# Moving row loads and feature stores from ScalarE's queue to SyncE's in a graph-attention and feed-forward kernel

## The chip, the cores and the metric

The kernel runs on one core of a Trainium2 chip. The metric is the device time of one execution in microseconds (us). The engines are TensorE (PE in the profile), VectorE (DVE), ScalarE (ACT), GpSimd (POOL) and SyncE (SP). SyncE does no arithmetic: it waits for semaphores and issues DMAs, one after the other, in program order. ScalarE can issue DMAs too, between its own instructions.

## What is computed

```python
x = x + gnn(layernorm(x), edge_index, ...)      # two graph-attention layers, 1250 nodes, 21250 edges
x = x + ffn(layernorm(x), ...)                  # GELU feed-forward, six class tokens with routed experts

def gat_layer(x, W, att_src, att_dst, bias, src, dst, heads, out_ch):
    h = (x @ W.T).reshape(n, heads, out_ch)
    e = leaky_relu(a_src[src] + a_dst[dst], 0.2)
    alpha = segment_softmax(e, dst)             # over the edges that end in one node
    return segment_sum(alpha * h[src], dst) + bias
```

The first layer has 8 heads of 128 channels (x is 1250x768, W1 is 1024x768).

## The kernel before

The edges are turned into a dense matrix. For each pair of nodes the kernel counts the edges and keeps the logarithm of the count; a softmax over a dense 1250x1250 matrix of logits plus log counts then replaces the segment operations. The 1250 nodes are worked on in `NT` = 10 tiles of `NP` = 125 rows.

The change lies in the first stage, roughly the first 145 us. For each tile t this stage does the following.

- **Rows.** `load_x(t)` loads 125 rows of x into `xin[t % 2]`. ScalarE takes the mean (`means`, L882), subtracts it (`centre`, L891) and sums the squares (L895). When L895 of tile t is done the semaphore `sq_ready` stands at t, and `xin[t % 2]` may be loaded again, with tile t+2. So `load_x(t + 2)` waits for `sq_ready` t.
- **Turning and products.** TensorE transposes the centred rows (`turn`, L1281), ScalarE copies them out of PSUM (`rows_turned`, L836 to L839), and `products(t)` (L1351) multiplies them with W1 in three passes.
- **Features.** `features_out(t)` (L864, L870) takes the result out of PSUM into `h1st[t % 2]`, with the semaphore `h1_out`. Its first piece frees the PSUM bank in which `products(t + 1)` begins (`h1_piece`). `store_h1(t)` stores `h1st[t % 2]` to the scratch tensor h1_d in DRAM; `features_out(t + 2)` waits until it has landed.
- **Counts.** `count_edges(t)` (L1268) counts the edges of a tile on TensorE with one-hot matrices that VectorE makes (L1968). `log_counts(t)` (L847) has ScalarE write the logarithms to `LCw[t % 2]`; VectorE mends them (`mend`, L1988, semaphore `lc_done`). SyncE stores them to DRAM (`store_lc(t)`, L478, 1250 pieces of 500 bytes, because the columns are re-ordered on the way) and loads them back row-wise (`load_lc(t)`, L485).

Two waits matter below. The first is at the head of `log_counts(t)`, a wait for the store of two tiles before, since it writes the same buffer:

```python
act.wait_ge(cnt_full, t + 1)
freed(act, lc_stored[t % 2], TWO * (t // 2))
```

The second is the program order of each engine: nothing is reordered by a scheduler, every engine runs the list written out by hand. On ScalarE one turn i of the loop at L939 is `features_out(i - 1)`, `rows_turned(i + 1)`, `means` and `centre` of tile i + 2, and `log_counts` at places set by hand: in turn 5 that of tile 5 comes right after `features_out(4)`, and that of tile 6 comes last, right ahead of `features_out(5)` in turn 6.

Each transfer of 125 rows is issued as two DMAs (`ROWS`: 112 rows and 13 rows).

Of the kernel before, what the change touches and what calls it, by code (L numbers as in the profile page):

```python
# [34 lines left out]
NP = 125  # L35
NT = N // NP
# [45 lines left out]
ROWS = ((0, CUT), (CUT, NP))  # L82
# [79 lines left out]
def gnn_ffn_kernel(nc, x, src_cols, dst_cols, dst_rows, W1, W1T, as1T, ad1T, b1c, W2, W2T, as2T, ad2T,  # L162
                   b2, fc1T, fc1b, fc2T, fc2b, gate_pair, atom_inT, atom_inb, atom_outT, atom_outb,
                   balance, out):
    h1_d = nc.dram_tensor("h1_scratch", (N, HC), F32).ap()
# [5 lines left out]
    with ctx:  # L171
        def sb(name, shape, dt=F32, where=ctx):
            return where.enter_context(nc.sbuf_tensor(name, shape, dt))

        def sem(name):
            return ctx.enter_context(nc.semaphore(name))
# [104 lines left out]
        xin = [sb("xin0", [NP, D], F32, p1)]  # L281
# [22 lines left out]
        h1st = [sb("h1st0", [NP, HC], F32, p1)]  # L304
# [105 lines left out]
        mean_step, sq_ready, h1_piece = (sem(n) for n in ("mean_step", "sq_ready", "h1_piece"))  # L410
        x_in = [sem(f"x_in{p}") for p in range(2)]
        stat_step, rstd_ready, xn_ready, xt_full, xT_ready = (
            sem(n) for n in ("stat_step", "rstd_ready", "xn_ready", "xt_full", "xT_ready"))
        logit_full, logit_rows, column_full, logit_done, h1_full, h1_out = (
            sem(n) for n in ("logit_full", "logit_rows", "column_full", "logit_done", "h1_full", "h1_out"))
        h1_stored = [sem(f"h1_stored{p}") for p in range(2)]
# [51 lines left out]
        def _(sp):  # L468
            def load_x(t):
                for a, b in ROWS:  # L470
                    sp.dma_start(xin[t % 2][a:b, :], x[t * NP + a:t * NP + b, :]).then_inc(x_in[t % 2], 16)

            def store_lc(t):

                sp.wait_ge(lc_done, t + 1)
                flat = lc_d.rearrange("n m -> (n m)")[t * NP * N:(t + 1) * NP * N]
                for a, b in ROWS:
                    sp.dma_start(flat.rearrange("(w p r) -> p w r", w=SUB, p=NP)[a:b, :, :],  # L478
                                 LCw[t % 2][a:b, :].rearrange("p (w r) -> p w r", w=SUB)).then_inc(lc_stored[t % 2], 16)

            def load_lc(t):

                sp.wait_ge(lc_stored[t % 2], TWO * (t // 2 + 1))
                for a, b in ROWS:
                    sp.dma_start(LC[a:b, t, :], lc_d[t * NP + a:t * NP + b, :]).then_inc(lc_in[t // 2], 16)  # L485

            def load_w2n(k):
                sp.dma_start(w2n_sb[:, k, :], W2[k * 128:(k + 1) * 128, :]).then_inc(w2n_in, 16)

# [15 lines left out]
            sp.dma_start(fc1b_sb[:, :], fc1b).then_inc(bias_in, 16)  # L505
            sp.wait_ge(sq_ready, 1)
            load_x(3)
            sp.wait_ge(wattp, 1)
            for k in range(KD):
                load_w2n(k)  # L510
            store_lc(0)
            for i in range(1, 8):
                store_lc(i)
                load_lc(i - 1)


            def load_features(q, h):
# [286 lines left out]
        def _(act):  # L804
# [26 lines left out]
            def rows_turned(t):  # L831
                p = t % 2
                act.wait_ge(xt_full, t + 1)
                if t > 2:
                    act.wait_ge(h1_full, t - 1)
                act.copy(xT[p][:, 0:4, :], bank[3][:, 0:4 * NP].rearrange("p (k n) -> p k n", k=4))  # L836
                act.copy(xT[p][:, 4:6, :], bank[4][:, 0:2 * NP].rearrange("p (k n) -> p k n", k=2))
                act.copy(xT_hi[p][:, 0:4, :], bank[3][:, 0:4 * NP].rearrange("p (k n) -> p k n", k=4))
                act.copy(xT_hi[p][:, 4:6, :], bank[4][:, 0:2 * NP].rearrange("p (k n) -> p k n", k=2)  # L839
                         ).then_inc(xT_ready, 1)  # L840

            def log_counts(t):
                act.wait_ge(cnt_full, t + 1)
                freed(act, lc_stored[t % 2], TWO * (t // 2))
                for b in range(3):
                    c0, c1 = b * 2 * GW, min((b + 1) * 2 * GW, N)
                    last = act.activation(LCw[t % 2][:, c0:c1], bank[b][0:NP, 0:c1 - c0], ACT.Ln,  # L847
                                          bias=tiny[:, 0:1], scale=2.0)
                last.then_inc(ln_done, 1)

            def features_out(t):
                act.wait_ge(h1_full, t + 1)
                freed(act, h1_stored[t % 2], TWO * (t // 2))
                pieces = THIRDS if t < FUSED else LAST_HALVES if t == NT - 1 else HALVES
                scale = 1.0
                if t in CENTRED:
                    act.wait_ge(rstd_ready, 2 * t + 1)
                    scale = rstd[:, t:t + 1]
                if t == NT - 1:
                    act.activation(h1s[0][:, t, :], bank[pieces[0][0]][0:NP, 0:C], ACT.Copy, scale=1.0  # L860
                                   ).then_inc(head_in[0], TWO)
                for b, c0, c1 in pieces:
                    c1 = min(c1, HC)
                    c = act.activation(h1st[t % 2][:, c0:c1], bank[b][0:NP, 0:c1 - c0], ACT.Copy, scale=scale)  # L864
                    if c0 != pieces[-1][1]:
                        c.then_inc(h1_piece, 1)
                if 0 < t < FUSED:
                    freed(act, rows_full, t - 1)
                    freed(act, col_done, t - 1)
                    c = act.activation(cols[t % 2][:, :], bank[5][0:NP, LOGIT0:LOGIT0 + 2 * H], ACT.Copy, scale=scale)  # L870
                c.then_inc(h1_out, 1)

            def centre_first():
                act.wait_ge(stat_step, 3)
                act.activation(xn[0][:, :], xin[0][:, :], ACT.Identity, bias=nmr[0][:, 0:1], scale=1.0).then_inc(xn_ready, 1)

            def means(t):
                p = t % 2
                act.wait_ge(x_in[p], TWO * (t // 2 + 1))
                act.wait_ge(stat_step, 4)  # L880
                freed(act, xt_full, t - 1)
                act.activation(xn[p][:, :], xin[p][:, :], ACT.Identity, bias=0.0, scale=1.0,  # L882
                               accum_out=mv[p][:, 0:1]).then_inc(mean_step, 1)
                act.wait_ge(mean_step, 2 * t - 1)
                act.activation(stats[p][:, 0, 0:1], mv[p][:, 0:1], ACT.Copy, scale=-1.0 / D).then_inc(mean_step, 1)
                act.wait_ge(mean_step, 2 * t)

            def centre(t):

                p = t % 2  # L890
                act.activation(xn[p][:, :], xin[p][:, :], ACT.Identity, bias=stats[p][:, 0, 0:1], scale=1.0  # L891
                               ).then_inc(xn_ready, 1)
                act.wait_ge(xn_ready, t + 1)
                freed(act, rstd_ready, 2 * t - 4)
                act.activation(xin[p][:, :], xn[p][:, :], ACT.Square, accum_out=mv[p][:, 1:2]).then_inc(sq_ready, 1)  # L895
# [7 lines left out]
            def store_h1(t):  # L903

                act.wait_ge(h1_out, t + 1)
                for a, b in ROWS:
                    act.dma_start(h1_d[t * NP + a:t * NP + b, :], h1st[t % 2][a:b, :]).then_inc(h1_stored[t % 2], 16)

            def load_x(t):

                act.wait_ge(sq_ready, t - 2)
                for a, b in ROWS:
                    act.dma_start(xin[t % 2][a:b, :], x[t * NP + a:t * NP + b, :]).then_inc(x_in[t % 2], 16)

            centre_first()
            first_turned()
            act.copy(iota2[:, :, 1], iota1[:, :]).then_inc(consts_made, 1)
# [12 lines left out]
            log_counts(0)  # L930
            means(2)
            centre(2)
            store_h1(0)
            load_x(4)
            rows_turned(2)
            means(3)
            centre(3)
            load_x(5)
            for i in range(2, NT):  # L939
                features_out(i - 1)  # L940
                if i in (2, 5):
                    log_counts({2: 1, 5: 5}[i])
                if i + 1 < NT:
                    rows_turned(i + 1)
                if i in (4, 7, 8):
                    log_counts({4: 4, 7: 8, 8: 9}[i])
                if i + 2 in CENTRED:
                    means(i + 2)
                    centre(i + 2)
                    if i + 4 < NT:  # L950
                        load_x(i + 4)
                elif i + 2 < NT:
                    normalise(i + 2)
                store_h1(i - 1)
                if FUSED <= i + 3 < NT:
                    means(i + 3)
                    squares(i + 3)
                if i in (2, 3, 5, 6):
                    log_counts({2: 2, 3: 3, 5: 6, 6: 7}[i])
                if i == NT - 2:  # L960
                    act.activation(early_exp[:, :], tiny[:, :], ACT.Exp)
# [1577 lines left out]
```

## Time and profile before

| | |
|---|---|
| median of 3 runs | 699.24 us (699.22 to 701.13) |
| the profiled execution, its own time | 699.48 us |
| span of its profile, first to last instruction | 697.5 us |
| TensorE busy | 685.4 us, 98% of the span |
| VectorE busy | 511.8 us, 73% |
| ScalarE busy | 441.1 us, 63% |
| DMA queue of SyncE (q1), share of 16 DMA engines | 32.2% |
| DMA queue of ScalarE (q10), share of 16 DMA engines | 6.0% |

The span is one execution, measured from its first to its last instruction; the execution's own time has about 2 us more around it. Busy shares are averages over stages with different limits. In the rows further down, ACTq and SPq are the DMA issues of ScalarE and of SyncE, and a time is microseconds from the start of the span.

### The profile page before, as it was taken

The page shows a single profiled execution, that of the slowest core. Times are in us where ns is not written, and L with a number is a line of the kernel's source. Part 1 is how long each engine was busy: PE and PEld are TensorE (multiplying, and loading weights), DVE is VectorE, ACT ScalarE, POOL GpSimd, SP SyncE. Part 2 cuts the span into 40 slices and gives each one's busy share as a digit, 9 for nine tenths or more (in the row PEclk, how much of TensorE's full clock was granted, in tenths as well). Part 3 has the DMA queues.
Part 4 walks back from the last instruction along what each step waited for, and adds up shares of the span by engine and source line. Part 5 has one row for each costly group of instructions (what it writes and reads, how often), then busy time and mean ns, then how long its engine had stood idle before and what let it go on. Part 6 is the DMA issues. An engine that isn't in the chain of part 4 may idle for free.

```text
span 697.5 us, 13734 instructions
## 1 busy us (share of the span) xinstructions
PE 685.4 (98%) x4749; PEld 644.8 (92%) x4749; DVE 511.8 (73%) x866; ACT 441.1 (63%) x900; POOL 126.3 (18%) x150
## 2 busy tenths in 40 slices
PE   7999999999999999999999999999999999999997
PEld 6799999889999999999999899999998999999997
DVE  7888875999899999999998854434668643837332
ACT  5767676388999999999999744454261424422202
POOL 2324120001021212112121000000242330333302
PEclk9999999999999999999999999999999999999999
DMA  8877886868434434343323231101963544315102
GB/s 286 252 255 211 198 220 161 205 194 275 82 72 84 101 57 99 70 81 90 58 22 79 73 106 60 59 1 52 318 206 117 159 137 162 95 59 188 32 23 69
DMA packets 54430, 88.37 MB, mean 127 GB/s; under 512 B 17763, under 2 KB 37081, under 8 KB 54378
## 3 DMA queue, kind: packets, MB, share of 16 engines
q1 hardware_dynamic: 43798, 65.69, 32.2%
q0 software_dynamic: 6080, 8.17, 7.4%
q10 hardware_dynamic: 4500, 13.82, 6.0%
q8 instruction: 31, 0.51, 0.3%
q14 instruction: 21, 0.17, 0.1%
HBM read 68.09 MB, written 15.33 MB: 120 GB/s over the span
## 4 chain that ended last, share of the span: by engine, by line
PE 87%; DVE 7%; ACT 2%; issue 2%; DVEq 1%; DMA 1%; POOL 0%; SPq 0%; ACTq 0%
PE bank L1495 19%; PE bank L1635 13%; PE bank L1456 12%; PE bank L1559 12%; PE bank L1351 10%; PE bank L1739 4%; PE bank L1711 3%; PE bank L1268 2%; PE bank L1613 2%; PE bank L1765 1%; DVE x2f L2392 1%; PE bank L1501 1%; PE bank L1502 1%; ACT w_hi L1054 1%; PE bank L1796 1%
## 5 line engine op out<-in xcount | busy, mean ns | idle before, releaser
L1495 PE MATMUL bank<-PT,h1s 125*128 125x250 f32 x660 | 147.5, 374 | 0.0
L1495 PEld LDWEIGHTS bank<-PT,h1s 125*128 125x128 f32 x660 | 121.2, 190 | 13.6
L2157 DVE SCALAR_TENSOR_TENSOR L<-asb,nad 125x1250 f32<-125x1250 f32 x80 | 121.3, 1552 | 1.5 <-DMA asb<-src_logit_rows 0.7
L2168 DVE CUSTOM_DVE_ANT_0 L<-L,LC 125x1250 f32<-125x1250 f32 x80 | 113.7, 1453 | 1.3
L969 ACT ACTIVATE L<-L,nm 125x1250 f32<-125x1250 f32 x80 | 109.7, 1373 | 6.1 <-DVE nm L2168 4.8
L1456 PE MATMUL bank<-ident,L 125*125 125x125 f32 x800 | 94.0, 273 | 0.0
L1456 PEld LDWEIGHTS bank<-ident,L 125*125 125x125 f32 x800 | 91.1, 189 | 0.8 <-issue 0.4
L990 ACT COPY PT<-bank 125x500 f32<-125x500 f32 x165 | 83.8, 619 | 2.7 <-PE bank L1456 2.7
L777 POOL DMA_DIRECT2D PT_diff<-PT x34 | 28.4, 837 | 158.9 <-ACT PT L990 158.9
L1968 DVE TENSOR_TENSOR hot<-iota,edges 125x750 f16<-125x750 f16 x100 | 46.9, 540 | 6.5 <-PE bank L1268 4.4
L1635 PE MATMUL bank<-h_hi,PT_hi 125*125 125x384 f32 x200 | 41.5, 350 | 0.0
L1635 PE MATMUL bank<-h_lo,PT_hi 125*125 125x384 f32 x200 | 40.5, 342 | 0.0
L1111 ACT ACTIVATE L<-L,nm 125x1250 f32<-125x1250 f32 x10 | 13.4, 1341 | 42.4 <-DVE nm L2312 42.4
L745 POOL TENSOR_TENSOR x<-x,b_sb 125x768 f32<-125x768 f32 x10 | 20.0, 1996 | 102.0 <-DMA fc2b_sb<-in_fc2b 92.3
L1635 PE MATMUL bank<-h_hi,PT_lo 125*125 125x384 f32 x200 | 38.1, 336 | 0.0
L1635 PEld LDWEIGHTS bank<-h_hi,PT_hi 125*125 125x125 f32 x200 | 34.0, 185 | 2.5 <-ACT PT_hi L1119 0.7
L1635 PEld LDWEIGHTS bank<-h_hi,PT_lo 125*125 125x125 f32 x200 | 35.2, 185 | 0.0
L1061 ACT ACTIVATE hT<-hT,b_sb x64 | 19.5, 387 | 24.7 <-DVE hT L2219 24.7
L2244 DVE COPY as2c<-bank 125x1 f32<-125x1 f32 x10 | 1.6, 159 | 45.6 <-ACT h_hi L1074 45.6
L1635 PEld LDWEIGHTS bank<-h_lo,PT_hi 125*125 125x125 f32 x200 | 34.9, 186 | 0.0
L2369 DVE TENSOR_TENSOR x2f<-bank,x2f 125x384 f32<-125x384 f32 x20 | 10.2, 552 | 29.6 <-PE bank L1739 27.9
L1559 PE MATMUL bank<-w_hi,h1Tt_hi 128*125 128x384 f32 (+1 forms) x160 | 31.0, 344 | 0.6 <-ACT w_hi L1054 0.5
(289 smaller groups left out, 1340.6 us busy)
## 6 DMA issues: line engine op xcount, KB each, us to landing
asb<-src_logit_rows SPq DMA_DIRECT2D x14, 416.5 KB, 3.5
atom_w<-in_atom_inT SPq DMA_DIRECT2D x5, 1152.0 KB, 12.2
atom_w<-in_atom_outT SPq DMA_DIRECT2D x5, 1152.0 KB, 9.7
log_count_scratch<-LCw SPq DMA_DIRECT2D x10, 546.9 KB
LC<-log_count_scratch SPq DMA_DIRECT2D x10, 546.9 KB
LCt<-log_count_scratch SPq DMA_DIRECT2D x10, 546.9 KB
h_scratch<-h1st ACTq DMA_DIRECT2D x10, 448.0 KB
PT_diff<-PT POOLq DMA_DIRECT2D x34, 122.1 KB, 3.0
```

Of the source, the lines that this page charges most:

```text
L777: pool.dma_start(PT_diff[p][:, :].bitcast(F32), PT[p][:, PART + 1, :], accum_op=ALU.add).then_inc(lower_moved[p], 16)
L969: e = act.activation(L[r][:, :], L[r][:, :], ACT.Exp, bias=nm[q][:, t:t + 1], scale=-1.0, accum_out=den[q][:, t:t + 1])
L990: act.copy(PT[(k - lag) % 2][:, 2 * b:2 * b + 2, :], turned[0:NP, 0:2 * GW].rearrange("p (s n) -> p s n", s=2)).then_inc(tb_evac, 1)
L1351: mm = pe.matmul(bank[b][0:NP, 0:c1 - c0], rows[t % 2][:, k, :], weights[:, k, c0:c1], start=(part == 0 and k == 0), stop=(part == 2 and k ...
L1456: mm = pe.transpose(bank[turned_bank(first, k - lag, b)][0:NP, (2 * s + j) * NP:(2 * s + j + 1) * NP], L[(2 * (k - lag) + j) % RING][:, (2 ...
L1495: mm = pe.matmul(sums, h1s[q][:, s, :], PT[p][:, s, :], start=(s == (0 if plain else PART + 2)), stop=(plain and s == NT - 1))
L1559: mm = pe.matmul(bank[2 * p + b][0:NP, 0:w], rows[p][:, k, :], weights[:, k, c0:c0 + w], start=(part == 0 and k == 0), stop=(part == 2 and ...
L1635: mm = pe.matmul(bank[2 + 2 * j + b][0:NP, 0:HALF], rows[:, s, j * NP:(j + 1) * NP], features[:, s, b * HALF:(b + 1) * HALF], start=(term ...
L1739: mm = pe.matmul(bank[down_bank(i, j) + b][0:NP, 0:HALF], rows[:, m, j * NP:(j + 1) * NP], weights[:, m, b * HALF:(b + 1) * HALF], start=( ...
L1968: made = dve.tensor_tensor(hot[w][:, :, :, :], iota2[:, w * NP:(w + 1) * NP, :].unsqueeze(1).to_broadcast([CE, VISIT, NP, 2]), edges[t % 2 ...
L2157: dve.scalar_tensor_tensor(L[s % RING][:, :], asb[q][0:NP, 1, :], nad1[:, ds(h, 1), t:t + 1].rearrange("p h t -> p (h t)"), asb[q][0:NP, 0 ...
L2168: dve.tensor_tensor_reduce(out=L[s % RING][:, :], in0=L[s % RING][:, :], in1=LC[:, t, :], scale=-1.0, scalar=-FLOOR, op0=ALU.add, op1=ALU.min,
```

## The change

ScalarE's `load_x` is gone: the row loads of tiles 4 to 9 are issued by SyncE, with the same condition on `sq_ready`. The feature stores of tiles 0 to 6 are issued by SyncE as well, with the same condition on `h1_out`; those of tiles 7 to 9 stay on ScalarE. SyncE's list of log-count stores and loads is woven together with them.

```diff
+            def load_next_x(t):
+                sp.wait_ge(sq_ready, t - 2)
+                load_x(t)
+
+            def store_h1(t):
+                sp.wait_ge(h1_out, t + 1)
+                for a, b in ROWS:
+                    sp.dma_start(h1_d[t * NP + a:t * NP + b, :], h1st[t % 2][a:b, :]).then_inc(h1_stored[t % 2], 16)
+
...
             sp.wait_ge(sq_ready, 1)
             load_x(3)
+            store_h1(0)
+            load_next_x(4)
             sp.wait_ge(wattp, 1)
             for k in range(KD):
                 load_w2n(k)
+            load_next_x(5)
+            store_h1(1)
             store_lc(0)
-            for i in range(1, 8):
-                store_lc(i)
-                load_lc(i - 1)
+            for i in range(2, 9):
+                if i + 4 < NT:
+                    load_next_x(i + 4)
+                if 2 < i < 8:
+                    store_h1(i - 1)
+                store_lc(i - 1)
+                load_lc(i - 2)
...
-            store_h1(0)
-            load_x(4)
             rows_turned(2)
             means(3)
             centre(3)
-            load_x(5)
             for i in range(2, NT):
                 features_out(i - 1)
...
                 if i + 2 in CENTRED:
                     means(i + 2)
                     centre(i + 2)
-                    if i + 4 < NT:
-                        load_x(i + 4)
                 elif i + 2 < NT:
                     normalise(i + 2)
-                store_h1(i - 1)
+                if i > 7:
+                    store_h1(i - 1)
```

On SyncE, before, the store of tile 3's log counts (`LCw1`) and that of tile 4 (`LCw0`) stand next to each other, with the load of tile 2 between them:

```order
L478 DMA log_count_scratch<-LCw1 112x10x125 [waits lc_done]
L478 DMA log_count_scratch<-LCw1 13x10x125
L485 DMA LC<-log_count_scratch 112x1250 [waits lc_stored0]
L485 DMA LC<-log_count_scratch 13x1250
L478 DMA log_count_scratch<-LCw0 112x10x125 [waits lc_done]
L478 DMA log_count_scratch<-LCw0 13x10x125
```

In the changed kernel (its line numbers differ: L471 loads rows of x, L494 stores features) the same place reads as follows, from the load of tile 8's rows to the feature store of tile 4; the store of tile 4's log counts comes right after it:

```order
L471 DMA xin0<-in_x 112x768 [waits sq_ready]
L471 DMA xin0<-in_x 13x768
L494 DMA h1_scratch<-h1st1 112x1024 [waits h1_out]
L494 DMA h1_scratch<-h1st1 13x1024
L478 DMA log_count_scratch<-LCw1 112x10x125 [waits lc_done]
L478 DMA log_count_scratch<-LCw1 13x10x125
L485 DMA LC<-log_count_scratch 112x1250 [waits lc_stored0]
L485 DMA LC<-log_count_scratch 13x1250
L471 DMA xin1<-in_x 112x768 [waits sq_ready]
L471 DMA xin1<-in_x 13x768
L494 DMA h1_scratch<-h1st0 112x1024 [waits h1_out]
L494 DMA h1_scratch<-h1st0 13x1024
```

The log-count stores of tiles 3 and 4 now each stand behind a wait for `sq_ready` and four more issues.

On ScalarE, before, turn 5 goes from the squares of tile 7 (L895) through four issues to the means of tile 8, its squares (L900) and the log counts of tile 6:

```order
L895 ACTIVATE xin1,mv1<-xn1 125x768 [waits rstd_ready,xn_ready]
L913 DMA xin1<-in_x 112x768 [waits sq_ready]
L913 DMA xin1<-in_x 13x768
L907 DMA h1_scratch<-h1st0 112x1024 [waits h1_out]
L907 DMA h1_scratch<-h1st0 13x1024
L882 ACTIVATE xn0,mv0<-xin0 125x768 [waits xt_full,stat_step,x_in0]
L885 ACTIVATE stats0<-mv0 125x1 [waits mean_step]
L900 ACTIVATE xn0,mv0<-xin0,stats0 125x768 [waits rstd_ready,mean_step]
L847 ACTIVATE LCw0<-bank0,tiny 125x500 [waits lc_stored0,cnt_full]
```

In the changed kernel the same instructions follow each other without the issues (L912 is the old L895, L864 the old L847):

```order
L912 ACTIVATE xin1,mv1<-xn1 125x768 [waits rstd_ready,xn_ready]
L899 ACTIVATE xn0,mv0<-xin0 125x768 [waits xt_full,stat_step,x_in0]
L902 ACTIVATE stats0<-mv0 125x1 [waits mean_step]
L917 ACTIVATE xn0,mv0<-xin0,stats0 125x768 [waits rstd_ready,mean_step]
L864 ACTIVATE LCw0<-bank0,tiny 125x500 [waits lc_stored0,cnt_full]
```

The wait for `lc_stored0` in front of the log counts has stayed where it was.

## Rows read from the trace of the kernel before

**Rows 1.** The page: busy time of TensorE, share of the span, instructions.

```profile
PE 685.4 (98%) x4749; PEld 644.8 (92%) x4749; DVE 511.8 (73%) x866; ACT 441.1 (63%) x900; POOL 126.3 (18%) x150
```

**Rows 2.** Busy time of each engine by stretch, then TensorE clock, DMA share, GB/s.

```profile
20.00:43.00 23.00, 21.24 (x223) 18.58 (x222) 17.32 (x39) 15.85 (x34) 6.68 (x6) 1.00 0.83 273
...
43.00:150.00 107.00, 106.17 (x856) 98.15 (x854) 88.04 (x167) 69.70 (x146) 19.55 (x16) 1.00 0.74 192
```

**Rows 3.** Timeline of TensorE at tile 6: start us, us, what.

```profile
91.56 0.81 PE L1281 MATMUL bank<-ident,xn 125*128 125x125 f32 x6
92.46 3.10 PE L1351 MATMUL bank<-w_hi,xT_hi 128*125 128x352 f32 x18
...
97.44 0.29 PE L1259 MATMUL bank<-iota,zeros 125*125 125x16 f16 x3
...
103.30 0.80 PE L1281 MATMUL bank<-ident,xn 125*128 125x125 f32 x6
```

**Rows 4.** Timeline of ScalarE, with its DMA issues (ACTq), turns 4 to 6.

```profile
76.10 0.79 ACTq L913 DMA_DIRECT2D xin<-in_x  x2
76.93 0.81 ACTq L907 DMA_DIRECT2D h_scratch<-h1st  x2
...
80.28 1.60 ACT L847 ACTIVATE LCw<-bank,tiny 125x500 f32<-125x500 f32 x3 [0.42 <-PE bank L1271]
...
86.19 0.18 ACT L895 ACTIVATION_READ_ACCUMULATOR xin<-xn 125x1 f32 x1
86.40 0.79 ACTq L913 DMA_DIRECT2D xin<-in_x  x2
87.22 0.80 ACTq L907 DMA_DIRECT2D h_scratch<-h1st  x2
88.15 0.85 ACT L882 ACTIVATE xn<-xin 125x768 f32<-125x768 f32 x1 [1.78 <-issue]
...
90.29 1.58 ACT L847 ACTIVATE LCw<-bank,tiny 125x500 f32<-125x500 f32 x3
91.76 1.42 ACT L864 ACTIVATE h1st<-bank,rstd 125x352 f32<-125x352 f32 x3
```

**Rows 5.** Timeline of SyncE: log-count stores of tiles 3, 4, 5 and 6.

```profile
69.63 0.93 SPq L478 DMA_DIRECT2D log_count_scratch<-LCw  x2
...
77.96 1.66 SPq L478 DMA_DIRECT2D log_count_scratch<-LCw  x2
...
87.00 0.96 SPq L478 DMA_DIRECT2D log_count_scratch<-LCw  x2
...
98.50 0.95 SPq L478 DMA_DIRECT2D log_count_scratch<-LCw  x2
```

**Rows 6.** DMA packets of 76.1:85.9, of 85.9:88.1, of 86.4:95.6, of 98.5:104.5.

```profile
DMA packets 1748, 2.16 MB, mean 220 GB/s; under 512 B 1371, under 2 KB 1371, under 8 KB 1747
...
DMA packets 56, 0.16 MB, mean 71 GB/s; under 512 B 10, under 2 KB 10, under 8 KB 56
...
DMA packets 1769, 2.29 MB, mean 248 GB/s; under 512 B 1363, under 2 KB 1363, under 8 KB 1767
...
DMA packets 1389, 1.14 MB, mean 190 GB/s; under 512 B 1287, under 2 KB 1287, under 8 KB 1388
```

**Rows 7.** Timeline of VectorE: tile 3's log counts are mended.

```profile
68.14 1.45 DVE L1988 SCALAR_TENSOR_TENSOR LCw<-LCw 125x1250 f32<-125x1250 f32 x1
```

**Rows 8.** Timeline of ScalarE, turn 2 to 3.

```profile
52.86 1.61 ACT L847 ACTIVATE LCw<-bank,tiny 125x500 f32<-125x500 f32 x3 [3.64 <-PE bank L1271]
54.81 1.42 ACT L864 ACTIVATE h1st<-bank,rstd 125x352 f32<-125x352 f32 x3 [0.34 <-PE bank L1351]
```

**Rows 9.** Timeline of TensorE at the start, and the last stretch by windows.

```profile
1.54 4.64 PE L1232 MATMUL bank<-ident 128*128 128x128 f32 x26 [1.54 <-POOL ident L693]
...
7.87 1.04 PE L1232 MATMUL bank<-ident 128*128 128x128 f32 x8
...
694.00:697.50 3.50, 0.00 (x0) 0.00 (x0) 0.55 (x2) 0.00 (x0) 0.00 (x0) 1.00 0.38 112
```

More of the change, by code:

```diff
@@ L907, in store_h1 @@
                     act.dma_start(h1_d[t * NP + a:t * NP + b, :], h1st[t % 2][a:b, :]).then_inc(h1_stored[t % 2], 16)
[L909 to L913, printed above, removed]
             centre_first()
```

## The prediction

> **What bounds the kernel now.** I read the page first: TensorE is busy for 685.4 of 697.5 us, so only idle time of TensorE can be won, and any new idle time is lost for good [rows 1]. Next I read the busy time by stretch, for the stage that the change touches. From 43 to 150 us TensorE is busy for 106.17 of 107 us; from 20 to 43 us for 21.24 of 23 [rows 2]. The whole stage holds 0.83 + 1.76 = 2.6 us to win. Then I read the timelines of ScalarE, SyncE and TensorE side by side, looking for places where one of them has just enough slack. The reader is to see two.
>
> The first is the edge between tiles 5 and 6. TensorE starts the products of tile 6 at 92.46 [rows 3], and needs for that the first piece of `features_out(5)`, which ScalarE begins at 91.76 [rows 4]. Between them lies the piece itself (1.42 / 3 is about 0.5 us) and some 0.2 us. So TensorE is hard behind ScalarE here. Ahead of that piece ScalarE has no idle time: `log_counts(6)` runs from 90.29 to 91.8, right up to it [rows 4]. Whatever delays `log_counts(6)` delays TensorE by the same.
>
> The second is the log-count buffer, of which there are two. `log_counts(5)`, at 80.28, may start when the store of tile 3 has landed, and `log_counts(6)`, at 90.29, when that of tile 4 has [rows 4]. Now these stores are issued at 69.63 and 77.96 [rows 5], as soon as the values are mended (tile 3 at 68.14 + 1.45 = 69.6 [rows 7]). They are done long before they are needed: the one of tile 4 by 85.9, since of the packets under 512 B 1371 start from 76.1 to 85.9 (1250 are the store's, the rest completion writes and strays) and only 10 in the 2.2 us after [rows 6].
>
> **The change part by part.** It removes 26 issues from ScalarE (two for each of 6 loads and 7 stores). At 0.79 to 0.81 us for a pair [rows 4] that is 13 x 0.8 = 10.4 us. Most of it lies in front of a wait for TensorE anyway. The clearest place is turn 5: four issues from 86.40 to 88.02 hold up the means of tile 8 by 1.78 us [rows 4]. Without them `log_counts(6)` could begin at 88.5. It gains TensorE nothing, since `features_out(5)` needs TensorE's own products of tile 5, which end when the turning at 91.56 starts [rows 3]. I cost the removal at 0.
>
> It adds the same 26 issues to SyncE, and that is no cost by itself: SyncE is idle for most of the stage. What costs is the order. `store_lc(3)` stood behind nothing; now it stands behind `load_next_x(8)`, which waits for `sq_ready` 6, that is for the moment 76.1 at which ScalarE issued this load before [rows 4]. Behind that come two issues of x and two of the feature store, 0.8 us each pair, so the store of tile 3 leaves at 77.7 instead of 69.63. In the same way `store_lc(4)` stands behind `load_next_x(9)`, which waits for `sq_ready` 7.
>
> Let L be the time from the issue of the row load to the end of the log-count store behind it. The trace has this group of three transfers (rows, features, log counts) twice. From 76.1 to 85.9 it took 9.8 us [rows 4, 6]; the second begins at 86.40, with the store at 87.00, and its 500-byte packets are through by 95.6 (1363), which makes 9.2 [rows 4 to 6]. A store with little beside it went from 98.50 to 104.5, 6.0 us [rows 5, 6]; 1.6 us behind the row load that makes L at least 7.6. I take 9.2, because the group of three is what will run, and the second had nothing held back within it.
>
> The steps are then:
>
> 1. Store 3 ends at 76.1 + L = 85.3. `log_counts(5)`, due at 80.28, starts 5.0 us late. TensorE doesn't feel it yet: the next thing it needs is tile 7, centred, at 91.56 [rows 3]; ScalarE is done with that tile at 86.4 now [rows 4], so by 91.4 then.
> 2. Everything behind it on ScalarE is 5.0 late, `sq_ready` 7 too: it comes at 86.4 + 5.0 = 91.4. This holds `load_next_x(9)`, and with it `store_lc(4)`, on SyncE.
> 3. Store 4 ends at 91.4 + 9.2 = 100.6. `log_counts(6)`, due at 90.29, starts 10.3 us late. The 1.7 us of issues that ScalarE no longer makes are swallowed by this wait.
> 4. `features_out(5)` begins at 102.1 and TensorE stands from about 92.4 to 102.8: **10.3 us**. In general the stall is 2L - 8.1, so 7.1 us at L = 7.6 and 11.5 at 9.8.
>
> What is late next: SyncE's `store_h1(5)` and `store_lc(5)` follow `features_out(5)`, 1.7 us after its start, and end some 8.5 to 10 us after it. `log_counts(7)` takes 1.6 more, up to 11.6, and `features_out(6)` is due after 11.7 (a tile of TensorE, 91.56 to 103.30 [rows 3]). That just fits. The same holds a tile further, for `normalise(9)`. Early in the stage the store of tile 0's log counts now queues behind the feature store of tile 1 and must land by 52.86, with 0.34 us to spare before TensorE is touched [rows 8]. For these three near misses together I take **0.5 us**, and 0 to 2 as bounds.
>
> A third term is TensorE's clock. The rows show a granted clock of 1.00, that is 2.4 GHz, in both stretches [rows 2], and it also stayed there during the 3.5 us at the end in which TensorE did nothing [rows 9]. No row shows what 10 idle microseconds do. At the very start 26 transposes took 4.64 us (178 ns each), and later 8 took 1.04 (130 ns) [rows 9]; a start like that costs 26 x 48 ns = 1.2 us, and a stretch of 4.64 us at half speed can cost at most 2.3. I take **1.0 us**, bounds 0 and 2.3. The Trainium skill says (TensorE: Matmul & The Clock Gate, Part 1) that an array that has idled falls back to 1.2 GHz and gets 2.4 GHz again only after sustained work; by that rule alone the fall is sure, and the term would be at its full 1.2 or more instead of 1.0.
>
> A rule speaks for the other side. The row load and the feature store had a queue of their own beside the store of the log counts, and the three together took 9.2 to 9.8 us against 6.0 for the store alone [rows 6], so the two queues already shared one transfer capacity. The Trainium skill says the same (DMA: Bandwidth & Descriptors, Issuing engines are not separate DMA queues): DMAs of different engines run on the same 16 DMA engines, and spreading them only saves issue time. Read alone it would have this change cost nothing and give ScalarE its 10.4 us; it is silent on waits in the issuing engine's own list, where my 10.3 us come from.
>
> Sum: 10.3 + 0.5 + 1.0 = 11.8 us on the profiled execution's 699.48 us, 711.3. The median of before is 0.24 lower, so 711.0.
>
> **The rivals.**
>
> *Only one link bites.* If ScalarE's wait in step 1 were short (L near 5), step 3 would nearly vanish: 2 x 5 - 8.1 = 1.9 us, 701. It needs a store that lands 3.4 us after its issue; the lone one took 6.0 [rows 6]. 5%.
>
> *The stores stay hidden, nothing changes.* This is so for L below 4.05, or if the delay of step 1 were made up by ScalarE before `sq_ready` 7. ScalarE has 0.42 us of idle time ahead of `log_counts(5)` [rows 4], and its instructions from there to 86.4 follow one another. The time would be 699 to 700. 6%.
>
> *Faster: ScalarE was the hidden brake.* Here TensorE's small gaps come from ScalarE being held up by its issues, as in the 1.78 us at 88.15 [rows 4]. The price is bounded by the idle time of the stage, 0.83 us after 43 and 1.76 before [rows 2]: 696.7 to 698.5. It decides if no store is late, so from L below 4.05 as well, and to be seen at all it would need most of the 2.6 us. 3%.
>
> *The clock falls and the queue is slower.* With one queue instead of two in flight, L may pass 9.8; at 10.5 the stall is 12.9, with 2.3 for the clock and 1 for near misses 715.4. 10%.
>
> My forecast (a stall of 7 to 12 us at the edge of tiles 5 and 6) has 76%.
>
> **How the numbers follow.** The likeliest value is 711.0. The forecast's own range is L from 7.6 to 9.8 with the smallest and the largest other terms: 699.2 + 7.1 = 706.3 and 699.2 + 11.5 + 3.8 = 714.5. To leave no more than 2 in 10 out I go a little beyond on both sides, 705 to 715. A change of 0.3%, 2.1 us, is about what a measurement can tell from none here. Faster holds 0.03; the hidden case and part of the one-link case give same 0.08; the rest, 0.89, is slower.
>
> **What the profile after would show.** Step 1: SyncE's store of tile 3 at about 77.7, and ScalarE's `log_counts(5)` near 85, with idle time ahead of it. Step 2: the row load of tile 9 on SyncE near 91. Step 3: `log_counts(6)` near 100 with 6 us or more of idle time before it. Step 4: one gap of TensorE of about 10 us between the turning of tile 7 (the transposes that start near 91.6) and the products of tile 6, and busy time of TensorE otherwise as before; the granted clock in the windows behind the gap tells the third term. I'd be wrong if `log_counts(5)` started by 82, if TensorE's gap lay elsewhere, or if the stretch after 150 us were longer by more than the clock explains.

## The result, and the profile after

The changed kernel takes 712.7 us (median of 5 runs, 712.4 to 712.98) against 699.71 us (5 runs) for the one before: ratio 1.0184, with an interval of 1.0173 to 1.0195. Its profiled execution took 712.54 us with a span of 710.7, that is 13.1 us and 13.2 us more than the one before. The first operation of the attention stage on TensorE starts 13.14 us later (149.26 us instead of 136.12), so nearly all of the loss lies ahead of that point.

The page of the changed kernel answers to [rows 1], its busy time by stretch to [rows 2].

```profile
PE 690.1 (97%) x4749; PEld 649.0 (91%) x4749; DVE 512.0 (72%) x866; ACT 441.1 (62%) x900; POOL 125.9 (18%) x150
```

```profile
20.00:43.00 23.00, 21.18 (x223) 18.55 (x221) 17.32 (x39) 15.50 (x35) 6.91 (x6) 1.00 0.84 287
43.00:150.00 107.00, 97.12 (x741) 91.17 (x742) 75.33 (x151) 56.97 (x123) 18.92 (x16) 0.95 0.67 169
```

From 43 to 150 us TensorE is now idle for 9.9 of 107 us instead of 0.8, and its granted clock has fallen from 1.00 to 0.95. The busy time of the whole page has grown by 4.7 us with the same 4749 instructions: the same work ran slower somewhere.

SyncE's timeline, with its DMA issues (SPq), shows the two links of the chain. Columns: start us, duration us, what. Line 471 is the row load, 494 the feature store, 478 the log-count store.

```profile
75.96 0.76 SPq L471 DMA_DIRECT2D xin<-in_x  x2
76.77 0.78 SPq L494 DMA_DIRECT2D h_scratch<-h1st  x2
77.60 1.83 SPq L478 DMA_DIRECT2D log_count_scratch<-LCw  x2
...
91.10 0.76 SPq L471 DMA_DIRECT2D xin<-in_x  x2
91.90 0.79 SPq L494 DMA_DIRECT2D h_scratch<-h1st  x2
92.73 1.96 SPq L478 DMA_DIRECT2D log_count_scratch<-LCw  x2
```

The log-count store of tile 3 left at 69.63 before, that of tile 4 at 77.96 [rows 5]. Now they leave at 77.60 and 92.73, each behind a row load that waits for ScalarE. ScalarE's timeline, answering to [rows 4], shows what that does to `log_counts(5)`, `log_counts(6)`, `features_out(5)` and, for tile 6's store, `log_counts(8)`.

```profile
84.98 1.60 ACT L864 ACTIVATE LCw<-bank,tiny 125x500 f32<-125x500 f32 x3 [5.26 <-DMA log_count_scratch<-LCw]
...
100.56 1.60 ACT L864 ACTIVATE LCw<-bank,tiny 125x500 f32<-125x500 f32 x3 [7.36 <-DMA log_count_scratch<-LCw]
102.04 1.42 ACT L881 ACTIVATE h1st<-bank,rstd 125x352 f32<-125x352 f32 x3
...
126.00 1.60 ACT L864 ACTIVATE LCw<-bank,tiny 125x500 f32<-125x500 f32 x3 [6.64 <-DMA log_count_scratch<-LCw]
```

The time in brackets is the idle time ahead, with what ended it: three times it is the landing of a log-count store. Before, 80.28 and 90.29 stood where 84.98 and 100.56 stand now, with 0.42 us of idle time and none. ScalarE's chain of waits sums it up.

```profile
ACT LCw L864 <- DMA log_count_scratch<-LCw: 19.3, 3, 7.4
```

And TensorE's timeline answers to [rows 3].

```profile
80.54 3.14 PE L1358 MATMUL bank<-w_hi,xT_hi 128*125 128x352 f32 x18
88.21 0.37 PE L1318 MATMUL bank<-ident,cols 125*8 125x125 f32 x1 [4.53 <-ACT xT_hi L856]
88.23 4.47 PE L1358 MATMUL bank<-w_lo,xT_hi 128*125 128x352 f32 x18
...
97.49 0.81 PE L1288 MATMUL bank<-ident,xn 125*128 125x125 f32 x6
102.75 5.54 PE L1358 MATMUL bank<-w_hi,xT_hi 128*125 128x352 f32 x18 [4.46 <-ACT h1st L881]
...
128.57 0.86 PE L1288 MATMUL bank<-ident,xn 125*128 125x125 f32 x6 [0.52 <-ACT xn L839]
```

The reader is to see two gaps, not one: 4.53 us inside the products of tile 5 and 4.46 us ahead of those of tile 6. Behind each stands a pass of 18 products that is slow: 4.47 and 5.54 us, where the kernel before took 3.12 and 3.10 for the same passes. The windows give the clock behind the second gap.

```profile
92.00:105.00 13.00, 8.54 (x71) 8.30 (x70) 4.85 (x11) 5.61 (x15) 1.11 (x4) 0.86 0.68 179
104.00:108.00 4.00, 4.00 (x15) 3.93 (x15) 0.00 (x0) 3.94 (x10) 0.00 (x0) 0.50 0.85 239
110.00:131.00 21.00, 20.39 (x192) 19.79 (x191) 14.43 (x28) 9.67 (x22) 2.27 (x2) 1.00 0.67 164
```

The granted clock of 0.50 is the lower of TensorE's two levels, 1.2 GHz. The sum closes. The products of tile 6 start at 102.75 instead of 92.46, 10.29 us late: 4.53 + 4.46 us of idle time and 4.47 - 3.12 = 1.35 us of slow clock behind the first gap make 10.3. Behind the second gap the clock adds 5.54 - 3.10 = 2.4. Ahead of the transposes at 128.57 TensorE waits 0.5 more. That makes 13.2.

The first gap comes from these two lines of TensorE's `logit_turn(t)`, which `products(5)` calls for t = 4 behind its first part:

```python
pe.wait_ge(h1_out, t + 1)
...
pe.wait_ge(xT_ready, t + 3)
```

`xT_ready` 7 means that `rows_turned(6)` is done, and on ScalarE that stands behind `log_counts(5)`. Before, the last cast of `rows_turned(6)` started at 82.94 and the transpose followed at 83.64; now 87.65 and 88.21.

### The profile page after: what moved, and what is told of

It is laid out like the page before. It is cut to its first block, busy times and chain, and to the rows that moved or that the text cites. A ratio compares the mean times of both kernels' runs of the same rounds, so it can differ in the third digit from the quotient of the medians.

```text
span 710.7 us, 13734 instructions
## 1 busy us (share of the span) xinstructions
PE 690.1 (97%) x4749; PEld 649.0 (91%) x4749; DVE 512.0 (72%) x866; ACT 441.1 (62%) x900; POOL 125.9 (18%) x150
## 4 chain that ended last, share of the span: by engine, by line
PE 82%; DVE 7%; DMA 3%; ACT 3%; issue 2%; DVEq 1%; SPq 1%; POOL 0%; ACTq 0%
PE bank L1502 19%; PE bank L1642 13%; PE bank L1463 12%; PE bank L1566 12%; PE bank L1358 7%; PE bank L1746 4%; PE bank L1718 3%; DMA log_count_scratch<-LCw 3%; PE bank L1620 2%; PE bank L1772 1%; DVE x2f L2399 1%; PE bank L1275 1%; PE bank L1508 1%; PE bank L1509 1%; ACT w_hi L1061 1%
## 5 line engine op out<-in xcount | busy, mean ns | idle before, releaser
L1358 PE MATMUL bank<-w_hi,xT_hi 128*125 128x352 f32 (+2 forms) x150 | 31.1, 360 | 5.6 <-ACT h1st L881 4.5
L864 ACT ACTIVATE LCw<-bank,tiny 125x500 f32<-125x500 f32 (+1 forms) x30 | 16.1, 611 | 31.5 <-DMA log_count_scratch<-LCw 19.3
## 6 DMA issues: line engine op xcount, KB each, us to landing
atom_w<-in_atom_inT SPq DMA_DIRECT2D x5, 1152.0 KB, 13.2
```

The lines of the kernel that those rows point to most:

```text
L1358: mm = pe.matmul(bank[b][0:NP, 0:c1 - c0], rows[t % 2][:, k, :], weights[:, k, c0:c1], start=(part == 0 and k == 0), stop=(part == 2 and k ...
```

## The experiments

**1. Is it the order on SyncE, or the move itself?** `k1_counts_first` keeps every moved issue on SyncE and only turns the order within a turn round.

```diff
             for i in range(2, 9):
-                if i + 4 < NT:
-                    load_next_x(i + 4)
-                if 2 < i < 8:
-                    store_h1(i - 1)
                 store_lc(i - 1)
                 load_lc(i - 2)
+                if 2 < i < 8:
+                    store_h1(i - 1)
+                if i + 4 < NT:
+                    load_next_x(i + 4)
```

Expected: 

> All row loads and feature stores stay on SyncE as in the change, but in each turn SyncE's log-count store and load come first, then the feature store, then the row load. Theory 1 (the loss is the wait for sq_ready and h1_out that stands in front of the log-count stores in SyncE's list): the store of tile 3 leaves near 69.6 and that of tile 4 near 78 us again, no late log_counts, no gap of TensorE, granted clock 1.00 throughout; 699.7 us, within 1 us. Rival 2 (one queue in place of two is slower for the same transfers): a loss stays, 703 us or more. Rival 3 (ScalarE freed of 26 issues gains something once the stores are in time): 698 us or less.

Measured: 699.21 us (12 runs, 699.04 to 700.13) against 699.56, ratio 0.9993 (0.9984 to 1.0003). Its windows and its timeline of ScalarE:

```profile
43.00:150.00 107.00, 106.18 (x856) 98.29 (x858) 88.54 (x168) 69.81 (x146) 19.36 (x16) 1.00 0.76 191
```

```profile
90.12 1.61 ACT L864 ACTIVATE LCw<-bank,tiny 125x500 f32<-125x500 f32 x3 [1.30 <-PE bank L1278]
92.09 1.42 ACT L881 ACTIVATE h1st<-bank,rstd 125x352 f32<-125x352 f32 x3 [0.36 <-PE bank L1358]
```

All of the loss is gone, so it is the order, and neither the queue nor the engine that issues. It also settles the rival in which ScalarE was the hidden brake: ScalarE has its issue time free here and spends it on waiting for TensorE (1.30 and 0.36 us ahead of the two steps), and the time doesn't move.

**2. Which of the moved transfers does it?** Two kernels move one kind each and leave the other on ScalarE.

```diff
 k2_stores_only: the stores as in the changed kernel, the row loads as before
-            load_next_x(4)
...
-            load_next_x(5)
...
-                if i + 4 < NT:
-                    load_next_x(i + 4)
 k3_loads_only: the row loads as in the changed kernel, the stores as before
-            store_h1(0)
...
-            store_h1(1)
...
-                if 2 < i < 8:
-                    store_h1(i - 1)
```

Expected of the first: 

> Only the feature stores of tiles 0 to 6 go to SyncE, in the place the change gave them; the row loads are ScalarE's again. Theory 1: the feature store waits for h1_out alone, which comes before lc_done in the turns of tiles 3 and 4, so the log-count stores leave near 69.6 and 80 us; 699.7 us, at most 1 us more. If the feature stores carry the loss: over 705 us.

Expected of the second: 

> Only the row loads of tiles 4 to 9 go to SyncE, in the place the change gave them; the feature stores are ScalarE's again. Theory 1: the wait for sq_ready alone is enough. The store of tile 3 leaves at 76.9 instead of 77.6 us and has the feature store beside it on the other queue; row load to end of store L is 8.4 to 9.2, so the products of tile 6 are 2L - 8.1 = 8.7 to 10.3 us late, and with the slow clock behind the gaps the time is 709 to 712.5 us. If the two moves share the loss evenly: about 706 us.

Measured: the stores alone 700.84 us (10 runs, 699.85 to 702.82), ratio 1.0013 (0.9999 to 1.0028); the loads alone 711.05 (4 runs), ratio 1.0152 (1.013 to 1.0174). The loads alone wait as the changed kernel does:

```profile
85.68 1.61 ACT L860 ACTIVATE LCw<-bank,tiny 125x500 f32<-125x500 f32 x3 [5.34 <-DMA log_count_scratch<-LCw]
101.39 1.61 ACT L860 ACTIVATE LCw<-bank,tiny 125x500 f32<-125x500 f32 x3 [7.40 <-DMA log_count_scratch<-LCw]
```

So the row load and the wait in front of it carry the loss. With the feature stores moved too the loss is 1.5 us larger by the medians and 2.2 us by the ratios (1.0184 against 1.0152, whose intervals just touch); by themselves they make no difference that can be told from none. In the kernel with the stores alone the timeline of ScalarE shows where they can bite: the log counts of tile 6 are stored behind its features.

```profile
114.05 1.61 ACT L860 ACTIVATE LCw<-bank,tiny 125x500 f32<-125x500 f32 x3 [6.77 <-DMA log_count_scratch<-LCw]
115.54 1.03 ACT L835 ACTIVATE xn<-xin,nmr,rstd 125x768 f32<-125x768 f32 x1
```

That is the near miss of `normalise(9)`. TensorE waited 0.65 us for it there. The traces split cleanly on this third link: in all eight profiles in which tile 6's log-count store stands behind its feature store on SyncE, TensorE waits 0.5 to 1.7 us ahead of the transposes of tile 9; in the five other kernels of the experiments (1, the loads alone, 3, and the two with tile 6 first), and in the kernel before, it doesn't wait there.

**3. The wait without any moved transfer.** `k6_wait_only` is the kernel before, with the moment of the wait alone copied to SyncE.

```diff
             for i in range(1, 8):
+                if i in (3, 4):
+                    sp.wait_ge(sq_ready, i + 3)
                 store_lc(i)
                 load_lc(i - 1)
```

Expected: 

> The kernel before, no DMA moved; only a wait for sq_ready 6 in front of SyncE's store of tile 3's log counts and for sq_ready 7 in front of that of tile 4. Theory 1 (the place in the list, not the traffic): stores leave at 76.1 and near 90 us, each takes about 8 us beside ScalarE's two transfers, TensorE stands in two places (the turning of tile 4's logits and the products of tile 6), and the time is 709 to 712 us. Rival 2 (the traffic of one queue): 700 us.

Measured: 711.15 us (4 runs, 708.28 to 712.41), ratio 1.0151 (1.0126 to 1.0177). Its TensorE:

```profile
82.83 3.07 PE L1353 MATMUL bank<-w_hi,xT_hi 128*125 128x352 f32 x18 [1.39 <-ACT h1st L866]
88.36 0.27 PE L1313 MATMUL bank<-ident,cols 125*8 125x125 f32 x1 [2.46 <-ACT xT_hi L841]
88.39 3.14 PE L1353 MATMUL bank<-w_lo,xT_hi 128*125 128x352 f32 x18
...
102.34 5.53 PE L1353 MATMUL bank<-w_hi,xT_hi 128*125 128x352 f32 x18 [5.22 <-ACT h1st L866]
```

Two waits on SyncE, with the kernel before otherwise unchanged, bring 11.6 of the 13 us. A slower single queue is excluded as the cause: here ScalarE still issues the loads and feature stores. The sharing of transfer capacity is not a rival but part of the price: log-count stores issued at 76.62 and 91.26 held ScalarE until 85.14 and 100.15, 8.5 and 8.9 us, beside ScalarE's transfers.

TensorE stands in three places here, not in the two that were expected. The added one, 1.39 us, comes from an issue on ScalarE ahead of `features_out(4)`:

```profile
77.60 4.40 ACTq L909 DMA_DIRECT2D h_scratch<-h1st  x2
```

In the kernel before, the same two issues took 0.81 us [rows 4]. In this run SyncE was issuing its load of log counts at the same time, from 77.61 for 4.37 us. Why the two held each other up is not shown.

**4. One link of the chain taken away.** `k5_one_link` lets the log-count store of tile 4 go ahead of the row load of tile 9.

```diff
             for i in range(2, 9):
+                if i == 5:
+                    store_lc(4)
                 if i + 4 < NT:
                     load_next_x(i + 4)
                 if 2 < i < 8:
                     store_h1(i - 1)
-                store_lc(i - 1)
+                if i != 5:
+                    store_lc(i - 1)
```

Expected: 

> The changed kernel, with one store moved: SyncE issues tile 4's log-count store ahead of the row load of tile 9 instead of behind it. Theory (two links, each adds one late store): the first gap stays, about 4.5 us and 1.4 us of slow clock behind it; log_counts(6) starts near 93 us instead of 100.6 and doesn't hold TensorE, so the second gap is gone; 705.5 to 706.5 us. Rival (only the second store matters): 700 us. Rival (only the first, the second follows from it in any order): 711 us or more.

Measured: 708.23 us (5 runs, 706.99 to 709.5), ratio 1.0108 (1.0074 to 1.0142). Its TensorE:

```profile
88.85 0.37 PE L1321 MATMUL bank<-ident,cols 125*8 125x125 f32 x1 [5.21 <-ACT xT_hi L859]
88.87 5.50 PE L1361 MATMUL bank<-w_lo,xT_hi 128*125 128x352 f32 x18
...
100.08 3.09 PE L1361 MATMUL bank<-w_hi,xT_hi 128*125 128x352 f32 x18
...
124.37 0.86 PE L1291 MATMUL bank<-ident,xn 125*128 125x125 f32 x6 [1.51 <-ACT xn L842]
```

The second gap is gone and the first one now counts in full: 5.21 + (5.50 - 3.12) + 1.51 = 9.1 us, and the attention stage starts 8.9 us late. The time is above what was expected by 2 us, because the first link had been priced at 4.5 us of gap and 1.4 us of slow clock and measured 5.21 and 2.4, and the wait at tile 9 was left out. One link costs 8.5 us, two cost 13: the links overlap, since a delay of the first gap is made up in the second wait.

**5. The clock, first try.** `k4_fill` is the changed kernel with products of zeros where TensorE would idle. `fill(bank, columns, count)` issues `count` products whose result, zero, is added to a bank.

```diff
+                    if t == 5 and part == 0:
+                        fill(6, 352, 28)
                     if t < FUSED and part == 0 and whole:
                         logit_turn(t - 1)
...
+                        if t == 5 and part == 2 and b == 5:
+                            fill(5, 320, 28)
```

Expected: 

> The changed kernel, with two groups of 28 added matrix products on TensorE that add zeros to a bank that is being accumulated: one ahead of the turning of tile 4's logits, one ahead of the last piece of the products of tile 5. Each lasts about 4.2 us and lies where TensorE now idles 4.5 us, so nothing that other engines wait for moves by more than 0.5 us. Theory (some 4 of the 13 us are the clock, which falls to 1.2 GHz in the gaps): the granted clock stays at 1.00, the passes behind the gaps take 3.1 us again instead of 4.5 and 5.5, and the time is 708.5 to 710 us. Rival (the slow passes come from something else, or the gap itself counts, not the idleness): 712.7 us, or more by the added work.

Measured: 713.68 us (4 runs, 712.12 to 714.17) against 699.77, ratio 1.0177 (1.0135 to 1.0219). The expectation was missed. Its TensorE:

```profile
83.76 4.34 PE L1336 MATMUL bank<-iota,zeros 125*125 125x352 f16 x28
...
89.21 3.10 PE L1367 MATMUL bank<-w_lo,xT_hi 128*125 128x352 f32 x18
...
96.16 3.97 PE L1336 MATMUL bank<-iota,zeros 125*125 125x320 f16 x28
...
104.63 4.32 PE L1367 MATMUL bank<-w_hi,xT_hi 128*125 128x352 f32 x18 [2.94 <-ACT h1st L881]
```

Behind the first fill the pass took 3.10 instead of 4.47 us, and that gained nothing: ScalarE, not TensorE, sets the start of tile 6. Behind the second, TensorE still idled for 2.94 us and the pass took 4.32. The log-count stores also landed later in this run: from row load to landed store it took 9.7 us (76.22 to 85.95) and 10.4 us (92.07 to 102.44), where the changed kernel's first profile has 9.0 and 9.5. The start of tile 6 is 1.9 us later than in that profile, more than the 1.2 us that its faster pass gave back.

**6. The same with tile 6's log counts sent first.** Three kernels on one chip: the changed kernel again, that kernel with `store_lc(6)` ahead of `store_h1(6)`, and the second with fills of 30 and 32 products at the places of experiment 5.

```diff
+                if i == 7:
+                    store_lc(6)
                 if 2 < i < 8:
                     store_h1(i - 1)
-                store_lc(i - 1)
+                if i != 7:
+                    store_lc(i - 1)
```

Expected of the changed kernel: 

> The changed kernel, unaltered, as the reference of the two kernels below on the same chip: 712 to 714 us, two gaps of TensorE of 4 to 5 us each, granted clock below 1.00 behind both.

Expected of tile 6 first: 

> The changed kernel, but in SyncE's last but one turn the log-count store of tile 6 is issued ahead of the feature store of tile 6. Theory (there is a third link: the store of tile 6 waits behind h1_out 7 and holds log_counts(8), normalise(9) and with them TensorE's turning of tile 9, 0.5 us in the profile of the changed kernel and 1.2 in that with the added products): TensorE no longer waits for L839, 0.5 to 1.0 us less than the changed kernel. Rival (this wait is TensorE's own lateness): no difference.

Expected with fills: 

> k8 with the added products that fill TensorE's two gaps, 30 and 32 of them instead of 28 and 28. Theory (the clock costs what it takes from the passes behind the second gap, 2.4 us; the slow clock behind the first gap is hidden in the second): where the filling reaches up to features_out(5) the clock stays at 1.00 and the kernel is 2 to 2.5 us faster than k8. Where the log-count stores land 1 to 2 us later than the filling lasts, only half of it. Rival (TensorE's clock isn't part of the loss): k8's time or more.

Measured: 712.99 (711.68 to 714.19), 711.68 (711.43 to 713.02) and 711.9 (710.06 to 712.29), 5 runs each, against 699.92. Tile 6 first takes the wait ahead of the last transposes away (0.57 us in the changed kernel's trace, none in this one), and the ratio falls from 1.0189 to 1.0172, with intervals that overlap (1.0173 to 1.0204, 1.0159 to 1.0186): as large as expected, but not shown by the times. The median shows nothing for the fills again. The timeline of TensorE with them shows why:

```profile
99.78 1.20 PE L1370 MATMUL bank<-w_hi,xT_lo 128*125 128x336 f32 x6
100.81 0.81 PE L1291 MATMUL bank<-ident,xn 125*128 125x125 f32 x6
103.92 4.64 PE L1370 MATMUL bank<-w_hi,xT_hi 128*125 128x352 f32 x18 [2.30 <-ACT h1st L884]
```

The gap was shorter, 2.30 us, and the pass behind it as slow as without fills (4.63 us). But this is one of the slower executions. Of the five, two kept a granted clock of 1.000 in the mean over the execution and took 710.06 and 710.32 us; the three with 0.996 to 0.998, the profiled one among them, took 711.9 to 712.29. `k4_fill` splits the same way: 712.12 us at 1.000, and 713.53 to 714.17 at 0.998.

The trace without fills, of `k8_tile6_first`, holds a fall of the clock that no gap of TensorE explains. Of the window from 36 to 40 us it shows:

```profile
36.00:40.00 4.00, 4.00 (x21) 3.85 (x20) 2.83 (x8) 2.10 (x5) 1.04 (x2) 0.60 1.02 406
```

TensorE was busy for all of it, and its largest idle stretches from 20 to 36 us were 1.01, 0.44 and 0.23 us. The kernel before has the clock at 1.00 in the same window. This costs about 1 us (from 34.27 to 44.60 us for what takes from 34.47 to 43.80 in the kernel before), and its cause stays open.

**7. The fill where the gap is.** The last three kernels ran on one chip: the changed kernel a third time, that kernel with a fill directly ahead of the transposes `turn(7)`, and that with a fill at both gaps. Here `fill` takes the first column as its second argument.

```diff
                 freed(pe, rows_out, t - 2)
+                if t == 7:
+                    fill(3, 0, 512, 19)
                 for k in range(KD):
...  (k11_both_fills alone)
+                    if t == 5 and part == 0:
+                        fill(6, 0, 352, 29)
```

Expected of the changed kernel: 

> The changed kernel once more, on the chip of the two kernels with fills beside it: 712.0 to 713.2, and in its trace two gaps of TensorE of 4.1 to 4.6 us, each followed by a first pass of products(6) or products(5) that takes 4.4 to 5.5 us instead of 3.1.

Expected of the late fill: 

> The changed kernel with 19 products of zeros (512 columns, f16, some 4.3 us) ahead of the transposes turn(7), so that TensorE idles for a few tenths ahead of products(6) instead of some 4.2 us. The first gap stays. The theory that the granted clock falls because of the idling (clock term, some 2.4 us behind the second gap): the first pass of products(6) is back at 3.1 to 3.5 us, the clock of the stretch from 104 to 110 at 0.95 or more, and the time 1.3 to 2.4 us below the changed kernel's. The theory that the clock falls there for another reason (as in the kernel that still idled for 2.3 us and got 0.72): pass at 4.4 to 4.6 us, and the changed kernel's time within 0.5 us.

Expected of both: 

> The same with 29 further products of zeros (352 columns, some 4.5 us) ahead of logit_turn(4), so that TensorE idles at neither place. If idling is what costs the clock: clock 1.00 over 76 to 131, both first passes at 3.1 us, and a time 2 to 2.6 us below the changed kernel's (some 710.3); what is left over the kernel before, some 10.5 us, is the waiting alone. The slow pass behind the first gap is by this theory hidden in the second wait, so the two kernels with fills differ by less than 0.6 us. If the clock falls for another reason, the time is the changed kernel's within 0.5 us.

Measured against 699.89: 715.54 (713.46 to 716.96, ratio 1.021, 1.019 to 1.0229), 713.48 (712.18 to 714.01 but for one execution of 1159.9 at a granted clock of 0.557, which the ratio leaves out, 1.0182, 1.0163 to 1.0201), and 714.49 (713.05 to 714.8, 1.0205, 1.0188 to 1.0223). The pass behind the second gap, in the changed kernel, with the late fill and with both:

```profile
105.68 5.53 PE L1358 MATMUL bank<-w_hi,xT_hi 128*125 128x352 f32 x18 [4.71 <-ACT h1st L881]
```

```profile
99.56 4.27 PE L1285 MATMUL bank<-iota,zeros 125*125 125x512 f16 x19
...
104.74 3.09 PE L1367 MATMUL bank<-w_hi,xT_hi 128*125 128x352 f32 x18 [0.27 <-ACT h1st L881]
```

```profile
97.39 4.26 PE L1285 MATMUL bank<-iota,zeros 125*125 125x512 f16 x19
...
104.92 3.10 PE L1367 MATMUL bank<-w_hi,xT_hi 128*125 128x352 f32 x18 [2.63 <-ACT h1st L881]
```

The slow pass is back at 3.09 us once TensorE is kept at work: here the idling is what costs the clock, and 2.4 us of pass is its price. The median is 2.1 us lower with the late fill, as expected, but the intervals of the ratios overlap a little. With both fills it is 1.0 lower, less than expected. The profiled execution there, 713.05 us, is the only one of five whose mean granted clock was 1.000; the other four had 0.997 or 0.998 and took 714.1 to 714.8. So in the three kernels with fills at both places (experiments 5, 6 and 7) four of fourteen executions kept the clock, and they took 1.5 to 1.9 us less than the mean of the others of their kernel. The fills kept the clock only sometimes, and the executions in which they did were the fastest of their kernel. How much of that is the clock, and how much stores that landed sooner, only traces of each could separate.

The changed kernel itself came out above its expected range on this chip. It took 10.0 us from row load to landed store both times (77.40 to 87.42, 93.53 to 103.49), where the first profile has 9.0 and 9.5; the row load of tile 8 left 1.4 us later than there, and the wait ahead of the transposes of tile 9 was 1.64 us instead of 0.52. In the kernel with the late fill that row load left at 76.29, so some 1 us of the distance between the two profiled executions arose ahead of the gaps and is not the clock's.

## Why the prediction was right, and where it was wrong

It gave 711.0 us, 705 to 715, and 712.7 came. The mechanism is the one it named, and experiments 1, 3 and 4 show it.

- *The price L.* Predicted 9.2. In the trace 75.96 to 84.98 and 91.10 to 100.56, 9.0 and 9.5 us. The formula 2L - 8.1 gives 10.4 with their mean, and the products of tile 6 were 10.29 late.
- *Step 1, the delay*: `log_counts(5)` 5.0 late at 85.3; 4.7 late at 84.98.
- *Step 1, "TensorE doesn't feel it yet": this is the step that failed.* The transpose in `logit_turn(4)` waits for `rows_turned(6)`, which stands behind `log_counts(5)`. Before, it had 0.3 us to spare: the cast at 82.94 takes 0.42 and the transpose starts at 83.64. So the predicted single gap of 10 us came as two of 4.5 us with 1.35 us of slow clock between. By the prediction's own sign ("if TensorE's gap lay elsewhere") it was wrong in this half. The total didn't change, because the start of tile 6 is set by the store of tile 4, whatever TensorE lost before; that the missed wait cost nothing is the luck of this chain. Where the second link is taken away and L stays above 9, the missed wait counts in full: 708 us in experiment 4. The prediction has no term for that case; its rival of one link, 701 us, is another one, with L near 5, which no run had.
- *Steps 2 to 4*: the load of tile 9 at 91.4, `log_counts(6)` at 100.6, `features_out(5)` at 102.1, TensorE at 102.8. Measured 91.10, 100.56, 102.04, 102.75.
- *The clock*, 1.0 with a bound of 2.3: mis-sized. It is 2.4 behind the second gap, and 1.35 to 2.4 behind the first that are hidden in the second wait. The loss is 13.0 us by the medians against 11.8 predicted, and the clock alone makes up for that; the other 0.5 us of the 1.7 is the kernel before, whose median was 699.24 over 3 runs when the forecast was made and is 699.71 over 5.
- *The near misses*, 0.5: 0.52 in the profile, all at the transposes of tile 9 behind tile 6's log-count store; 0.5 to 1.7 over the eight profiles with that order.
- *The removal*, costed at 0: confirmed by experiment 1, to within 0.7 us (ratio from 0.9984 to 1.0003). `log_counts(6)` could not have begun at 88.5, though: with the issues gone and the stores in time it waited 1.30 us for TensorE's counts of its tile and began at 90.12.
- *The range*: with 2 us for the near misses and 2.3 for the clock, the largest other terms are 4.3 and not 3.8, and the forecast's own upper end 715.0 and not 714.5. The stated range holds it either way.

## What to carry to other kernels

Before moving a DMA issue to an engine that looks idle, write down what each issue waits for and what stands behind it in that engine's order: a transfer that must leave early may not stand behind one that waits for a later event. If the move is wanted, put the issues that are ready first, as experiment 1 did, and expect no more than the idle time that the bounding engine has. When you follow a delay downstream, list every wait of the bounding engine, the small transposes too, and price the lowered clock behind each gap.

## What the runs showed of the hardware

- Behind gaps of TensorE of 3.8 to 5.8 us a pass of 18 products took 4.4 to 5.5 us instead of 3.1, thirteen times of thirteen, in eight profiles; in the window from 104 to 108 us of the changed kernel's first profile the granted clock was 0.50, that is 1.2 GHz. By contrast, the 3.5 us of idle time at the end had shown 1.00 [rows 9], with no product behind it to time.
- The length of the gap alone doesn't tell: behind 2.30 us of idle time the pass took 4.64 us (experiment 6), behind 2.94 us 4.32 (experiment 5), but behind 2.63 us 3.10 (experiment 7, where a longer fill lay directly ahead of the transposes and the gap) and behind 2.46 us 3.14 (experiment 3, without any fill). In one profile the clock fell with no idle stretch above 1.01 us near (experiment 6). What makes the difference stays open.
- The group of row load, feature store and log-count store took 9.0 to 10.4 us on one queue over the profiles here, about as on two (9.2 and 9.8 [rows 6], 9.1 and 9.6 in the kernel with the loads alone). It varied by up to 1 us within one kernel.
- A pair of DMA issues of ScalarE that takes 0.81 us in the kernel before took 4.40 us while SyncE was issuing too (experiment 3).
